# Tile 0 of a gated long-convolution and mixture-of-experts kernel, split into pieces at the start of the program

## The reference

```python
# x, ctx (8, 256, 512): 8 batches, 32 heads of 8 channels, 512 positions
kv = einsum('bhil,bhjl->bijhl', ctx, ctx)          # products of channel pairs
y  = irfft(rfft(kv, 1024) * rfft(ssm_kernel, 1024))[..., :512]   # causal conv per head
out = y + kv * D                                   # D: one number per head
out = einsum('bijhl,bhil->bjhl', out, layernorm(x))
x = x + tanh(g_xattn) * out
t = layernorm(x)
# 16 experts of width 352, the best 2 of softmax(t @ gate_w.T) per row, and a shared expert of width 704:
x = x + tanh(g_ffn) * (sum_e w_e * swiglu_e(t) + swiglu_shared(t))
```

## Time and profile before

| | before |
|---|---|
| median of 3 runs | 751.05 us (749.33 to 751.97) |
| the profiled execution, its own time | 753.55 us |
| its span, first to last instruction | 751.7 us |
| PE busy | 719.3 us, 96% |
| DVE, ACT, POOL busy | 565.8, 459.8, 371.6 us |
| DMA | 114.88 MB in 47716 packets, 153 GB/s over the span |

### The profile page before, as it was taken

One profiled execution on the slowest core, in us unless ns is written; L12 is line 12 of the kernel. 1 busy time (PEld: TensorE's weight loads), 2 busy tenths in 40 slices (PEclk: granted clock), 3 DMA queues, 4 the chain that ended last, 5 costly groups with the idle time before them and its releaser, 6 DMA issues.

```text
span 751.7 us, 15536 instructions
## 1 busy us (share of the span) xinstructions
PE 719.3 (96%) x4602; PEld 677.8 (90%) x4602; DVE 565.8 (75%) x1107; ACT 459.8 (61%) x657; POOL 371.6 (49%) x189
## 2 busy tenths in 40 slices
PE   1899999999999999999998999999998999999998
PEld 1899999999989999899997999988997999999997
DVE  4699898989865569427897489848997689769942
ACT  5657576666432322226887479748986698678941
POOL 2989888888401156032353435425644445534320
PEclk9999999999999999999999999999999999999999
DMA  6767877778521212462566578775656764332101
GB/s 183 246 203 224 265 229 256 246 246 251 178 105 58 43 31 47 107 203 55 183 181 151 162 204 259 205 206 122 162 154 182 188 177 112 73 60 57 44 1 56
DMA packets 47716, 114.88 MB, mean 153 GB/s; under 512 B 7424, under 2 KB 7424, under 8 KB 47648
## 3 DMA queue, kind: packets, MB, share of 16 engines
q1 hardware_dynamic: 35104, 89.67, 36.4%
q0 software_dynamic: 12544, 24.40, 17.2%
HBM read 157.78 MB, written 29.26 MB: 249 GB/s over the span
## 4 chain that ended last, share of the span: by engine, by line
PE 59%; DVE 13%; DMA 12%; issue 7%; ACT 4%; SPq 2%; DVEq 1%; ACTq 1%; POOL 1%; POOLq 0%
PE pair L1242 16%; PE bank L1242 12%; PE pair L1267 10%; PE pair L1178 7%; DMA out<-ys,slot_info 7%; PE bank L1267 5%; PE bank L1136 3%; PE pair L1250 3%; DMA raw<-in_weights 2%; PE bank L1189 2%; DVE prod L785 2%; DVE rows L797 2%; DVE bank L790 2%; DVE x L756 2%; DVE st L736 1%
## 5 line engine op out<-in xcount | busy, mean ns | idle before, releaser
L1101 DVE TENSOR_TENSOR w_lo<-raw,w_hi 128x1408 fp32r<-128x1408 f32 x94 | 149.0, 1623 | 47.4 <-ACT w_hi L693 47.2
L1379 POOL DMA_INDIRECT out<-ys,slot_info x47 | 89.5, 1905 | 121.3 <-DMA out<-ys,slot_info 58.4
L693 ACT ACTIVATE w_hi<-raw 128x1408 fp32r x94 | 124.9, 1374 | 11.9 <-DMA raw<-in_weights 10.0
L1366 POOL DMA_INDIRECT tn<-t_rows,slot_info x47 | 72.5, 1542 | 118.9 <-DVE tT_lo L839 82.8
L1178 PE MATMUL pair<-kv_hi,toep_hi 128*128 128x288 f32 x320 | 101.1, 316 | 0.9 <-issue 0.9
L1178 PE MATMUL pair<-kv_lo,toep_hi 128*128 128x288 f32 x320 | 95.8, 299 | 0.0
L1178 PE MATMUL pair<-kv_hi,toep_lo 128*128 128x288 f32 x320 | 95.6, 299 | 0.0
L1106 DVE TENSOR_TENSOR w_lo<-raw,w_hi 128x1536 fp32r<-128x1536 f32 x47 | 82.4, 1753 | 11.3 <-ACT w_hi L700 11.3
L1321 POOL TENSOR_TENSOR kv_lo<-kv,kv_hi 128x2304 fp32r<-128x2304 f32 (+1 forms) x16 | 79.6, 4978 | 16.4 <-ACT kv_hi L607 16.4
L700 ACT ACTIVATE w_hi<-raw 128x1536 fp32r x47 | 69.3, 1474 | 7.0 <-DMA raw<-in_weights 6.9
L785 DVE TENSOR_TENSOR prod<-pair,q 128x256 f32<-128x256 f32 x128 | 53.5, 418 | 15.2 <-PE pair L1178 9.9
(11 more groups left out here) (220 smaller groups left out, 1976.9 us busy)
## 6 DMA issues: line engine op xcount, KB each, us to landing
raw<-in_weights SPq DMA_DIRECT2D x94, 704.0 KB
raw<-in_weights SPq DMA_DIRECT2D x47, 768.0 KB
toep_hi<-kpad_hi SPq DMA_DIRECT2D x16, 512.0 KB, 4.3
toep_lo<-kpad_lo SPq DMA_DIRECT2D x16, 512.0 KB, 6.2
cx<-in_ctx SPq DMA_DIRECT2D x16, 384.0 KB, 6.2
stage<-in_weights SPq DMA_DIRECT2D x16, 272.0 KB, 6.6
xt<-in_x SPq DMA_DIRECT2D x16, 256.0 KB, 6.3
xr<-in_x SPq DMA_DIRECT2D x16, 256.0 KB, 6.6
```

Of the source, the lines that this page charges most:

```text
L693: act.activation(w_hi[s % 2][:, a:b], raw[:, bass.ds(half + a, b - a)], ACT.Copy).then_inc(hi_ok[n_], 1)
L1101: dve.tensor_tensor(w_lo[s % 2][:, a:b], raw[:, bass.ds(half + a, b - a)], w_hi[s % 2][:, a:b].bitcast(F32), ALU.subtract).then_inc(lo_ok[ ...
L1366: pool.indirect_dma_start(out=tn[o % 2][:], out_offset=None, in_=t_rows, in_offset=bass.IndirectOffsetOnAxis(ap=slot_info[:, 3 * i:3 * i + ...
L1379: pool.indirect_dma_start(out=out, out_offset=bass.IndirectOffsetOnAxis(ap=rows, axis=0), in_=ys[o % 2][:], in_offset=None, bounds_check=R ...
```

## The change: what it does

- SP's first DMAs come in another order: kernel rows and D first, without a wait; then the gates, the first quarter of tile 0's `cx` (blocks 0), `xt`, the rest of `cx`. Tile 1's `cx` is issued ahead of the Toeplitz loads. These come as four pieces: block diagonal 0 of hi and lo (128x2x128 each, semaphore `toep_first`), then the other three (128x2x384 each).
- DVE clears only the edges of `krow`, and rounds `krow_hi` itself (a copy of 32x640, in place of ACT's). It forms the first 576 columns of tile 0's kv, then the rest, and makes all of tile 0's `kv_lo` in three pieces (576, 576, 1152 columns). ACT rounds `kv_hi` in the same three pieces, with the square in two, and with `std_x(0)` and `norm_x(0)` between them.
- PE's `conv(0, 0)` waits only for `toep_first` and the first piece, `conv(0, 1)` for all Toeplitz rows and the second, `conv(0, 2)` for the third.
- POOL no longer has a part in tile 0's kv; it clears the two `prod` buffers (DVE did), then forms tile 1's kv. In its turn 0 `split_kv(1)` stands ahead of `split_shared(0)`. In ACT's turn 0 `std_x(1)` and `split_kv_hi(1)` stand ahead of `split_shared(0)`, and `square(1)` ahead of `q_copy(0)`.
- The turns of tiles 1 to 15 and stage two are as they were.

The core of the diff:

```diff
         def _(sp):
-            sp.dma_start(cx[0][:], ctx_ext[0]).then_inc(ctx_in[0], 16)
-            sp.dma_start(gts[:], gates).then_inc(gates_in, 16)
-            sp.wait_ge(setup_dve, 1)
             sp.dma_start(krow[:, P - 1:P - 1 + L], conv_rows).then_inc(kpad_in, 16)
             sp.dma_start(drow[:], conv_d).then_inc(kpad_in, 16)
+            sp.dma_start(gts[:], gates).then_inc(gates_in, 16)
+            sp.dma_start(cx[0][:, 0:2 * GW], ctx_ext[0][:, 0:2 * GW]).then_inc(ctx_first, 16)
             sp.dma_start(xt[0][:], x_t[0]).then_inc(x_in[0], 16)
+            sp.dma_start(cx[0][:, 2 * GW:], ctx_ext[0][:, 2 * GW:]).then_inc(ctx_in[0], 16)
             sp.wait_ge(krowh_ok, 1)
...
-            load(At(0), "toep")
             load(At(1), "ctx")
+            sp.wait_ge(kpadh_out, 16)
+            sp.wait_ge(kpadl_out, 16)
+            for a, b, landed in ((0, P, toep_first), (P, L, toep_in[0])):
+                for part, rows in ((toep_hi, toeplitz[0]), (toep_lo, toeplitz[1])):
+                    sp.dma_start(part[0][:].bitcast(F32).rearrange("p (h c) -> p h c", h=2)[:, :, a:b],
+                                 rows[0][:, :, a:b]).then_inc(landed, 16)
             load(At(1), "x")
...
-            square(At(0))
-            act.wait_ge(kpad_ok, 1)
-            act.activation(krow_hi[:], krow[:], ACT.Copy).then_inc(krowh_ok, 1)
-            split_kv_hi(At(0))
+            act.wait_ge(ctx_first, 16)
+            square_rows(0, 0, 2, square_first)
...
+            first_kv_hi(0, 1, kvh_first)
+            act.wait_ge(ctx_in[0], 16)
+            square_rows(0, 2, BLOCKS * 2 - 2, square_ok)
             std_x(At(0))
...
+            first_kv_hi(1, 2, kvh_first)
             norm_x(At(0))
+            first_kv_hi(2, BLOCKS, kvh_ok)
+            square(At(1))
             q_copy(At(0))
-            square(At(1))
 
             def turn(t):
                 first, last = t.within(0, 1), t.within(TILES - 1, TILES)
+                if first:
+                    std_x(t + 1)
+                    split_kv_hi(t + 1)
                 split_shared(t)
-                if not last:
+                if not first and not last:
                     split_kv_hi(t + 1)
                     std_x(t + 1)
...
+            dve.tensor_copy(krow_hi[:], krow[:]).then_inc(krowh_ok, 1)
...
-            form(dve, At(0))
-            dve.memset(prod[0][:], 0.0).then_inc(setup_dve, 1)
+            dve.wait_ge(ctx_first, 16)
+            pair_rows(dve, 0, 0, 2, kv_first)
+            dve.wait_ge(ctx_in[0], 16)
+            pair_rows(dve, 0, 2, BLOCKS * 2 - 2, kv_ok)
+            dve.wait_ge(kvh_first, 1)
+            first_kv_lo(0, 1, kvl_first)
             scale_x(At(0))
-            dve.memset(prod[1][:], 0.0).then_inc(setup_dve, 1)
-            split_first_kv()
+            dve.wait_ge(kvh_first, 2)
+            first_kv_lo(1, 2, kvl_first)
+            dve.wait_ge(kvh_ok, 1)
+            first_kv_lo(2, BLOCKS, kvl_ok)
...
-            split_kv(At(0))
+            for part in prod:
+                pool.memset(part[:], 0.0).then_inc(setup_pool, 1)
+            pool.wait_ge(kv_ok, 2)
             form(pool, At(1))
 
             def turn(t):
                 if not t.within(TILES - 2, TILES):
                     form(pool, t + 2)
+                if t.within(0, 1):
+                    split_kv(t + 1)
                 split_shared(t)
-                if not t.within(TILES - 1, TILES):
+                if not t.within(0, 1) and not t.within(TILES - 1, TILES):
                     split_kv(t + 1)
```

More of the change, by code:

```diff
@@ L51 @@
 SLOTS = SLOT_TILES + 1
-KV_DVE = 1280
+KVB = 2 * BATCH * PAIRS
 STAGE = SHARED * WROW // TILES
@@ L723, in _ @@
         def _(dve):
-            dve.memset(krow[:], 0.0).then_inc(setup_dve, 1)
+            dve.memset(krow[:, 0:P - 1], 0.0).then_inc(setup_dve, 1)
+            dve.memset(krow[:, P - 1 + L:], 0.0).then_inc(setup_dve, 1)
             dve.memset(small[:, 0:1], EPS).then_inc(setup_dve, 1)
@@ L729, in _ @@
             dve.tensor_tensor(krow[:, P - 1:P], krow[:, P - 1:P], drow[:], ALU.add).then_inc(kpad_ok, 1)
+            dve.wait_ge(setup_dve, 4)
+            dve.wait_ge(kpad_ok, 1)
+            dve.tensor_copy(krow_hi[:], krow[:]).then_inc(krowh_ok, 1)
             dve.wait_ge(krowh_ok, 1)
@@ L797, in products, with first_kv_lo @@
                 dve.tensor_tensor(rows[par][:], ps_rows, prod[par][:, 0:L], ALU.add).then_inc(rows_ok, 1)
[L799 to L803, removed]
+            def first_kv_lo(a, b, ok):
+                dve.tensor_tensor(kv_lo[0][:, a * KVB:b * KVB], kv[0][:, a * KVB:b * KVB],
+                                  kv_hi[0][:, a * KVB:b * KVB].bitcast(F32), ALU.subtract).then_inc(ok, 1)
             def logits_copy(t):
@@ L1167, in conv @@
                         if lb == 0:
-                            wait(pe, toep_in[p], (t.half() + 1) * 32)
                             if t.within(0, 1):
-                                pe.wait_ge(kvl_ok, 1)
-                            wait(pe, kvl2_ok, t + 1)
+                                pe.wait_ge(toep_first, 32)
+                                pe.wait_ge(kvl_first, 1)
+                            else:
+                                wait(pe, toep_in[p], (t.half() + 1) * 32)
+                                wait(pe, kvl_ok, t + 1)
+                        if t.within(0, 1) and lb == 1:
+                            pe.wait_ge(toep_in[0], 32)
+                            pe.wait_ge(kvl_first, 2)
+                        if t.within(0, 1) and lb == 2:
+                            pe.wait_ge(kvl_ok, 1)
                         wait(pe, prod_ok, (t * 4 + lb - 1) * PROD_STEPS)
@@ L1319, in split_kv @@
                 wait(pool, kvh_ok, t + 1)
-                a = KV_DVE if t.within(0, 1) else 0
-                pool.tensor_tensor(kv_lo[t.odd][:, a:], kv[t.odd][:, a:], kv_hi[t.odd][:, a:].bitcast(F32),
-                                   ALU.subtract).then_inc(kvl2_ok, 1)
-            split_kv(At(0))
+                pool.tensor_tensor(kv_lo[t.odd][:], kv[t.odd][:], kv_hi[t.odd][:].bitcast(F32),
+                                   ALU.subtract).then_inc(kvl_ok, 1)
+            for part in prod:
+                pool.memset(part[:], 0.0).then_inc(setup_pool, 1)
+            pool.wait_ge(kv_ok, 2)
             form(pool, At(1))
```

64 lines of the change are left out of this document (38 added, 26 removed).

## The result

The changed kernel took 747.76 us (median of 22 executions) against 751.85 for the kernel before (22): a ratio of 0.9942, 95% interval 0.9927 to 0.9958, or 4.4 us less (3.2 to 5.5). The forecast was 6.6 us less, from 751.05 to 744.4. The 751.05 was the median of three executions; over 22 the kernel before took 0.8 us more. Applied to 751.05 the ratio gives 746.7 us, inside the stated range of 742.0 to 747.7; the 747.76 itself lies 0.06 us above its slow end. The gain of 4.4 us is less than the 5.0 to 7.8 that the bounds of the forecast's terms gave. In a later comparison one execution of each kernel took several times as long (2530.51 and 4050.76 us), and these two are left out of all ratios.

What follows compares the result with a forecast made beforehand. PE was taken to set stage one's pace once `conv(2, 0)` begins; the start-up chain through POOL moves that mark from 44.14 to 37.5, 6.6 us, so the median goes from 751.05 to 744.4 us, range 742.0 to 747.7.

Steps and rivals of the forecast that it cites:

- Kernel rows: Start-up: D as second DMA, so `kpad_lo` is stored at 5.6 to 5.7 and landed at 7.4 instead of 9.5.
- Toeplitz rows: Start-up loads: last row landed at 14.4 instead of 15.66, with 0.8 us for extra pieces and `cx(1)`.
- Rival A: Toeplitz loads: short pieces are slow, rows land up to 4.6 us later, near 18; gain 3, 748.1; chance 0.12.
- PE in tile 0: `conv(0, 0)` near 12.1, 0.9 us of waiting, `conv(0, 1)` at 14.4, 3.3 us earlier; transposes and sum done at 25.3.
- POOL to `conv(1, 0)`: `cx(2)` lands at 16.2, the subtraction ends at 25.5, `conv(1, 0)` starts at 25.6, 6.0 us earlier; both arms nearly level.
- To `conv(2, 0)`: Tile 1: PE needs 11.1 us, POOL's `kv_lo(2)` is ready at 37.4 and sets `conv(2, 0)` at about 37.5, not 44.14.
- The opening claim: Stage one: PE sets the pace, waiting 0.9 us from 44 to 200 us; moving `conv(2, 0)` moves the end equally.
- Rival B: Later tiles of stage one: the early start is given back to POOL or DMA limits, 751; chance 0.10.
- The bounds of the gain: Start-up: term 1 at its bounds and term 2 from 13.6 to 15.6 give a gain of 5.0 to 7.8.
- term 1: The kernel rows step: `kpad_lo` landed at 7.4, bounds 6.0 to 7.8.
- term 2: The Toeplitz rows step: last landing at 14.4, taken from 13.6 to 15.6 for the bounds.
- Rival C: Tiles 0 and 1: short waits keep PE at 1.2 GHz, `conv(2, 0)` 6.8 us later, 757.8; chance 0.03.

Runs made afterwards that it cites:

- a_toep_whole: Changed kernel with tile 0's Toeplitz rows in two whole loads, for which `conv(0, 0)` waits; ratio 0.9908 (0.9877 to 0.9939).
- a_late_kv1: Changed kernel with `cx(1)` behind the Toeplitz loads and turn 0's orders on ACT and POOL as before; ratio 0.9940 (0.9916 to 0.9963).
- b_kv_sooner: Kernel before with `cx(1)` ahead of the Toeplitz loads and turn 0's orders on ACT and POOL as in the change; ratio 0.9931 (0.9906 to 0.9957).
- a_again: Changed kernel, unedited, second profile and comparison; ratio 0.9927 (0.9897 to 0.9957), 5.5 us less than the kernel before.
- a_third: Changed kernel, unedited, third profile and comparison; ratio 0.9926 (0.9900 to 0.9953), 5.6 us less than the kernel before.
- a_pool_order: Changed kernel with tile 0's shared split back ahead of tile 1's subtraction on POOL; ratio 0.9948 (0.9921 to 0.9976).
- b_third: Kernel before, unedited, third profile; ratio to itself 0.9985, as in the other repeat.
- a_gate_quarter: Changed kernel without three of each tile's four gate matmuls; one execution, read for stage one only: `conv(1, 0)` to `conv(2, 0)` 12.07 us.

## Why the prediction was right, and where it was not

1. *Kernel rows.* Forecast: `kpad_lo` stored at 5.7, landed 7.4. Measured 4.50 and 7.2. D landed sooner and the rounding took 0.48, but the store took 2.7 us instead of 1.7, behind `cx` and `xt`. Two errors that cancelled.
2. *Toeplitz rows.* 14.4 forecast, 14.3 measured. I had put 0.8 us on the extra pieces and `cx(1)` together, and from the first issue to the last landing it took 7.0 to 7.5 us in three profiles, against 6.0 to 6.2 in three of before. How this divides is not settled. With `cx(1)` ahead, whole loads (a_toep_whole, 7.3) are no faster than pieces. But with the pieces, `cx(1)` behind (a_late_kv1, 7.0) is no faster than `cx(1)` ahead either; its `conv(0, 1)` at 13.86 comes from the store, which landed at 6.8 instead of 7.2. And on the kernel before, with whole loads, `cx(1)` ahead made it 7.8 (b_kv_sooner). So either of the two costs 0.8 us or more when it stands alone, and both together no more than one. Rival A is excluded: `conv(0, 1)` began at 13.9 to 14.8, not after 17. The rule of the Trainium skill on 512 B ("DMA: Bandwidth & Descriptors", Specifications) agrees with a_toep_whole; that `cx(1)` is what remains, as the prediction drew from it, a_late_kv1 does not show.
3. *PE in tile 0.* 0.9 us of waiting forecast, 1.3 measured, `conv(0, 1)` within 0.1 us. (Before, it began at 17.87, not at the 17.73 of the sum.)
4. *POOL to `conv(1, 0)`.* 25.6 forecast, 25.49 measured, with `kv_lo(1)` at 25.39 as the releaser, so too in a_again (25.88, and 25.98). In a_third POOL was done at 25.01 and PE, with no gap in its list, began at 25.45: the two arms are as level as the forecast said. What I left out is that form(1) and DVE's `kv_lo` hold each other up. It cost DVE 3.2 us and was covered by the wait for the Toeplitz rows.
5. *To `conv(2, 0)`.* This step failed, though its number was met. I took 11.1 us for tile 1 on PE and let POOL set 37.5. a_pool_order, with POOL ready 1.5 us ahead and the mark at 39.27, shows that POOL does not set it: tile 1 takes 12.06 by a chain that runs 3 us over DVE's products and residual and 9 over PE; 25.49 + 12.06 = 37.55. POOL's number, 37.3 measured, lay close to it by luck. The 11.1 came from counting the clock's fall at 1.4 us. Its real price was 12.56 - 12.06 = 0.5 us, because PE at full clock has to wait for the residual, and most of its loss was under that wait. b_third, where the lower clock lasted 6.8 us instead of 3.4, took 13.45 us for the tile, 1.4 more. So the moved shared split has no price at `conv(2, 0)` but a gain: 1.7 us (39.27 against 37.55), the whole of what it brings `conv(1, 0)`. POOL is just 0.25 us from being the bound, though.

*The opening claim* that PE sets the pace of stage one was half right. PE hardly waits, but a_gate_quarter shows that shorter work on PE buys nothing where DVE's residual is level with it. The conclusion drawn from it, that whatever moves `conv(2, 0)` moves the end, holds in the profiles up to the start of stage two (6.4 of the 6.6 us), and behind it within their scatter: 606.5 to 607.6 us on average from `conv(2, 0)` on.

*The size.* 6.6 us forecast, 6.6 on the marks, 4.4 to 5.6 in three comparisons of the times. The step that is off is the last one, from the mark to the median, if it is not chance. Rival B in its full form is excluded; that 0.25 us is given back in stage one is shown, and more in stage two is neither shown nor excluded. The bounds of the gain were summed wrongly at one end: term 1 can be 1.4 us sooner and term 2 0.8, which makes 8.8 at most, not 7.8.

*Rival C.* PE waited 1.3 us ahead of `conv(0, 1)` and did not stay at the lower clock: the granted clock in tile 1 was 1.00. The example that the prediction took from the Trainium skill ("TensorE: Matmul & The Clock Gate", HAM oscillation) has waits of several microseconds in every round, so it gave little ground for rating this rival higher.

## What to carry to other kernels

The wait that ends last sets a stage, and where two engines are almost level, work taken from one of them can return as a wait for the other; an experiment that takes the work away tells this in one profile, and a busy share of 99% does not. It tells it for that place in the list only. A start-up is a race of chains: count the landing of each load and what stands ahead of it in the queue, and do not expect the parts of a change to add up. A number that is met is not yet a mechanism that is right; move one of the two candidates by itself. And a mark in a profile is not yet a time: here a part of the change moved its mark by less than half of the whole, and the times of part and whole could not be told apart.

## What the runs showed of the hardware

- When DVE subtracts with two operands in SBUF while POOL multiplies with two, one of them is held up: DVE 3.40 and 1.87 us instead of 0.76 and 1.36, or POOL 5.18 instead of 3.5. The held one ended about its own length, or a little less, after the other's instruction.
- The lower clock after a gap is not a matter of the gap's length alone: gaps of about 4 us with transposes in them brought 3.4 us at 1.2 GHz in two profiles of the kernel before and 6.8 in the third, and nothing in the profile of a_late_kv1. Of a_late_kv1's eight executions four have a mean granted clock of 0.999 or more; of 102 of the kernel before none is over 0.998.
- A small store of 80 KB took 1.7 us with no load just ahead of it and 2.2 to 3.3 us behind 640 KB of loads on the same queue.
